# A new order of work for the first stage of an attention and mixture-of-experts layer

## The reference, cut to what matters

```python
h = tok(x)                                  # 128 batches of (375, 512): q, k, v are 125 rows each
#   weight = softmax(q.T k / sqrt(125)) over 512 positions; h = v weight.T       -> (128, 125, 512)
h = h + attn(layernorm(h), Wq, Wk, Wv, Wo)  # 8 heads of 64, 2 key/value heads, rope, softcap 50
y = layernorm(h)
h = h + (silu(y @ sw1) * (y @ sw3)) @ sw2   # shared expert, inner width 448
scores = softmax(y @ gate_w); sel = top_2(scores + expert_bias)   # 8 experts, 16000 tokens
h = h + sum over the two experts e in sel of
        (silu((y*s_e) @ w1[e]) * ((y*s_e) @ w3[e])) @ w2[e]
```

## Time and profile before

| | |
|---|---|
| median of 3 runs | 5918.14 us (5916.59 to 5921.06) |
| the profiled execution | 5922.86 us, its span 5921.1 us |
| busy of the span | PE 98%, PEld 85%, DVE 75%, ACT 52%, POOL 35% |
| first stage | about the first 62% of the span |
| second stage | about the last 37% |

### The profile page before, as it was taken

How to read it: one execution, slowest core, us unless ns; L and a number is a source line. 1 busy time by engine, 2 the same in 40 slices (tenths; PEclk the granted TensorE clock), 3 DMA queues, 4 the chain that set the end, 5 groups by cost and what they waited for, 6 DMA issues and landing times. The chain is left out here.

```text
span 5921.1 us, 109291 instructions
## 1 busy us (share of the span) xinstructions
PE 5784.0 (98%) x32259; PEld 5009.4 (85%) x32259; DVE 4450.0 (75%) x10104; ACT 3084.8 (52%) x5748; POOL 2101.8 (35%) x1711
## 2 busy tenths in 40 slices
PE   5999999999999999999999997899999999999999
PEld 4888888888888888888888886899999999999998
DVE  4888888888888888888888886666666766666665
ACT  3555555555555555555555553555555555555554
POOL 1333333333333333333333332333434444444343
PEclk8999999999999999999999999999999999999999
DMA  2111111111111111111111111777777777777762
GB/s 73 47 50 44 44 49 46 43 47 49 43 45 50 44 44 49 46 43 47 49 43 45 50 44 25 190 188 187 184 189 182 182 187 188 183 189 182 184 167 79
DMA packets 363663, 565.45 MB, mean 95 GB/s; under 512 B 92898, under 2 KB 187106, under 8 KB 363492
## 3 DMA queue, kind: packets, MB, share of 16 engines
q1 hardware_dynamic: 294276, 433.22, 24.2%
q0 software_dynamic: 69344, 131.70, 11.3%
HBM read 438.14 MB, written 138.42 MB: 97 GB/s over the span
## 5 line engine op out<-in xcount | busy, mean ns | idle before, releaser
L1438 POOL DMA_INDIRECT out_dram<-res,goal x273 | 560.8, 2054 | 1070.4 <-DMA entries<-routed_entries 480.8
L930 POOL TENSOR_SCALAR ve<-ag 125x1 f32<-125x1 f32 x256 | 56.1, 219 | 1618.3 <-DVE ag L755 942.2
L639 ACT ACTIVATE e<-ps,negmax 128x512 f32<-128x512 f32 x512 | 348.6, 685 | 513.5 <-PE ps L449 409.8
L1188 PE MATMUL ps<-rT_hi,up_hi 128*128 128x384 f32 x2548 | 552.3, 338 | 1.6 <-DVE rT_lo L1348 1.6
L1188 PE MATMUL ps<-rT_lo,up_hi 128*128 128x384 f32 x2548 | 552.1, 338 | 0.0
L1188 PE MATMUL ps<-rT_hi,up_lo 128*128 128x384 f32 x2548 | 552.0, 338 | 0.0
L1278 ACT ACTIVATE uT_hi<-egb 128x384 fp32r<-128x384 f32 x364 | 191.4, 526 | 572.3 <-DVE egb L1367 561.5
L1188 PEld LDWEIGHTS ps<-rT_hi,up_hi 128*128 128x128 f32 x2548 | 457.8, 188 | 9.8 <-issue 2.0
L1188 PEld LDWEIGHTS ps<-rT_lo,up_hi 128*128 128x128 f32 x2548 | 456.3, 188 | 0.0
L1188 PEld LDWEIGHTS ps<-rT_hi,up_lo 128*128 128x128 f32 x2548 | 456.2, 188 | 0.0
L942 POOL TENSOR_TENSOR qk_low<-X,qk_high 125x1024 fp32r<-125x1024 f32 x128 | 306.3, 2393 | 345.7 <-ACT qk_high L626 345.7
(11 more groups left out here) (220 smaller groups left out, 15549.2 us busy)
## 6 DMA issues: line engine op xcount, KB each, us to landing
raw<-in_L_ffn_w SPq DMA_DIRECT2D x182, 768.0 KB, 5.1
X<-in_x SPq DMA_DIRECT2D x128, 750.0 KB
raw<-in_L_ffn_w SPq DMA_DIRECT2D x91, 896.0 KB
raw<-in_L_ffn_w SPq DMA_DIRECT2D x273, 128.0 KB, 5.0
normed_rows<-y SPq DMA_DIRECT2D x128, 250.0 KB
out_dram<-h SPq DMA_DIRECT2D x128, 250.0 KB
rows<-normed_rows,entries POOLq DMA_INDIRECT x273
out_dram<-res,goal POOLq DMA_INDIRECT x273
```

Source lines behind the costliest of these rows:

```text
L639: nc.scalar.activation(e[:, i, :], ps[:, (i + 1) % 2, :], ACT.Exp, bias=negmax[:, i:i + 1], accum_out=total[:, i:i + 1]).then_inc(e_sb.sem, 1)
L1188: ins = nc.tensor.matmul(ps[:, bank, 0:GROUP], w[a][:, k, col:col + P], rT[b][:, k, :], start=(k == 0 and i == 0), stop=(k == KC - 1 and i ...
L1438: nc.gpsimd.indirect_dma_start(out, bass.IndirectOffsetOnAxis(ap=goal[group[1] % 2][:, i:i + 1], axis=0), res[i][:], None, bounds_check=la ...
```

## The change

It writes the streams of all five engines in the first stage in a new order. The same sums are computed.

- **PE:** the upper product, `attend(0)`, `attend(1)`, the inner turns, the whole down product and the ranks of a batch are issued one step later than before. The new order is: scores 0 and 1; upper product of `g`; scores 2 and 3; turns of v and `xn`; `attend(0)`, `attend(1)` of `f`; query product; inner turns of `g`; turn of `attn`; weights turns 0 and 1; key/value product; output product; weights turns 2 and 3; down product of `g` (11 matmuls); ranks; rope turns; high blend; turn of `y`; attention scores; low blend; gate product of `f`.
- **ACT:** the gate's tanh and the router's exp come first in the next step; the four scalings of `e`, so far on DVE, are now ACT's, after `vT_full`; the rounding of the next batch stands ahead of `e_cut_hi` 2 and 3; tanh of the attention is taken in place.
- **DVE:** gate and routing chain move to the start of the next step, between the maxima and `xT_lo`; the normalisation of `attn` follows; the second norm comes after rope; entries and places stand at the end of the step.
- **POOL:** the order is now `rstd(a)`, `vT_low`, rope sum, `rstd(f)`, `cut_scores`, scatters.
- **SP:** `y` is stored ahead of `h3`.
- The second buffer of `vaug` and the tiles `qkr` and `capped` go; some banks change.

The diff, cut to its core (PE, ACT, DVE, POOL in this order):

```diff
+                    if has(3):
+
                         pe.wait_ge(tanh_sb.sem, tanh_sb.at(f))
-                        turn(5, P, attn[:, :, :].rearrange("p a b -> p (a b)")).then_inc(aT_ps.sem, 1)
-                    if has(3):
-                        down_part(0, 1)
-                        down_part(1, 1)
+                        product(pe, ps[0:C, 7, 0:HID], yT, w3s, P, 0, HID, yT_lo.sem, yT_lo.at(g)).then_inc(up_ps.sem, 1)
+                    if has(0):
+                        scores(2)
+                        scores(3)
...
+                    if has(1):
+
+                        pe.wait_ge(xn_sb.sem, xn_sb.at(a))
+                        pe.wait_ge(place.sem, place.at(back(g, 1)))
+                        turn(3, xn).then_inc(xT_ps.sem, 1)
+                    if has(2):
+
+                        pe.wait_ge(v_sb.sem, v_sb.at(f))
+                        pe.wait_ge(gb_sb.sem, gb_sb.at(g))
+                        attend(0)
+                        pe.wait_ge(ga_sb.sem, ga_sb.at(g))
+                        attend(1)
+                    if has(1):
+
+                        pe.wait_ge(yT_lo.sem, yT_lo.at(g))
+                        pe.wait_ge(xT_hi.sem, xT_hi.at(a))
+                        product(pe, ps[0:C, 4, :], xT, wqkv, P, 0, D, xT_lo.sem, xT_lo.at(a)).then_inc(q_ps.sem, 1)
...
+                        pe.wait_ge(gb_sb.sem, gb_sb.at(g))
+                        pe.wait_ge(vT_sb.sem, vT_sb.at(t))
+                        for k in range(3):
+                            nc.tensor.transpose(ps[:, 2, k * C:(k + 1) * C], gb[0:C, k * P:(k + 1) * P],
+                                                ident[0:C, 0:C])
+                        nc.tensor.transpose(ps[0:TAIL, 2, 3 * C:4 * C], gb[0:C, 3 * P:HID],
+                                            ident[0:C, 0:C]).then_inc(hT_ps.sem, 1)
+                    if has(2):
+
+                        pe.wait_ge(attn_sb.sem, attn_sb.at(f))
+                        pe.wait_ge(xT_lo.sem, xT_lo.at(a))
+                        turn(3, attn[:, :, :].rearrange("p a b -> p (a b)")).then_inc(aT_ps.sem, 1)
+                    if has(0):
+                        turn_weights(0)
+                        turn_weights(1)
+                    if has(1):
+
+                        pe.wait_ge(tanh_sb.sem, tanh_sb.at(f))
+                        product(pe, ps[0:C, 5, 0:QKV - D], xT, wqkv, P, D, QKV, xT_lo.sem, xT_lo.at(a)).then_inc(kv_ps.sem, 1)
                     if has(2):
 
                         pe.wait_ge(aT_hi.sem, aT_hi.at(f))
                         product(pe, ps[0:C, 7, :], aT, woT, P, 0, D, aT_lo.sem, aT_lo.at(f)).then_inc(wo_ps.sem, 1)
-                    if has(1):
-
...
-                        product(pe, ps[0:C, 7, 0:HID], yT, w3s, P, 0, HID, yT_lo.sem, yT_lo.at(f)).then_inc(up_ps.sem, 1)
+                    if has(3):
+
+                        pe.wait_ge(attn_sb.sem, attn_sb.at(f))
+                        pe.wait_ge(hT_hi.sem, hT_hi.at(g))
+                        for part in range(2):
+                            for k in range(3):
+                                down_part(k, part)
+                        pe.wait_ge(hT_lo.sem, hT_lo.at(g))
+                        for part in range(2):
+                            down_part(3, part)
+                        for k in range(3):
...
                         last.then_inc(rT_ps.sem, 1)
                     if has(0):
 
@@ -567,19 +567,19 @@
                                 blend(j, 0, b)
                     if has(2):
...
+                    def soften(kv):
+
+                        act.wait_ge(s_ps.sem, s_ps.at(a, kv + 1))
+                        act.wait_ge(pv_ps.sem, pv_ps.at(f))
+                        nc.scalar.activation(prob[0:C, kv, :], ps[0:C, 5 + 2 * kv, 0:G * C], ACT.Tanh,
+                                             scale=TANH).then_inc(tanh_sb.sem, 1)
+                        act.wait_ge(tanh_sb.sem, tanh_sb.at(a, kv + 1))
+                        nc.scalar.activation(prob[0:C, kv, :], prob[0:C, kv, :], ACT.Exp,
+                                             scale=CAPF).then_inc(p_sb.sem, 1)
...
+                        act.wait_ge(rz_sb.sem, rz_sb.at(t))
+                        for i in range(KC):
+                            nc.scalar.activation(e[:, i, :], e[:, i, :], ACT.Copy,
+                                                 scale=rz[:, i:i + 1]).then_inc(e_norm.sem, 1)
...
+                    if has(-1):
+                        round_scores(back(t, -1))
                     if has(0):
                         weights_hi(2)
                         weights_hi(3)
-
-                    if has(-1):
-                        round_scores(back(t, -1))
...
+                        act.wait_ge(yT_ps.sem, yT_ps.at(f))
+                        act.wait_ge(up_ps.sem, up_ps.at(g))
+                        hi_part(yT, 4).then_inc(yT_hi.sem, 1)
+                    if has(1):
+                        soften(0)
                     if has(0):
                         act.wait_ge(o_ps.sem, o_ps.at(t))
                         act.wait_ge(h2_sb.sem, h2_sb.at(f))
                         nc.scalar.activation(h[p][0:C, :], ps[0:C, 0, :], ACT.Copy).then_inc(h_sb.sem, 1)
+                    if has(1):
+                        soften(1)
                 each_step(act, step)
...
+                    if has(3):
+                        dve.wait_ge(th_sb.sem, th_sb.at(g))
+                        dve.wait_ge(pick.sem, pick.at(back(g, 1)))
+                        nc.vector.tensor_reduce(nl[0:C, :], ps[0:C, 6, HID:HG], AX.X, ALU.max,
+                                                negate=True).then_inc(nl_sb.sem, 1)
+                    if has(0):
+                        maxima(0)
...
+
+                        dve.wait_ge(ex_sb.sem, ex_sb.at(g))
+                        nc.vector.scalar_tensor_tensor(ga[0:C, :], th[0:C, :], 1.0, ps[0:C, 6, 0:HID],
+                                                       ALU.add, ALU.mult).then_inc(ga_sb.sem, 1)
+                        dve.wait_ge(ga_sb.sem, ga_sb.at(g))
+                        dve.wait_ge(up_ps.sem, up_ps.at(g))
+                        dve.wait_ge(hT_ps.sem, hT_ps.at(back(g, 1)))
+                        nc.vector.scalar_tensor_tensor(gb[0:C, :], ga[0:C, :], 0.5, ps[0:C, 7, 0:HID],
+                                                       ALU.mult, ALU.mult).then_inc(gb_sb.sem, 1)
                     if has(0):
...
+                        chosen(nc.vector.reciprocal(rse[0:C, :], se[0:C, :]))
+                        chosen(nc.vector.tensor_scalar(sc[0:C, :], ex[0:C, :], rse[0:C, :], None, ALU.mult))
+                        chosen(nc.vector.tensor_tensor(met[0:C, :], sc[0:C, :], bias_t[0:C, :], ALU.add))
...
+                        dve.wait_ge(rank_ps.sem, rank_ps.at(back(g, 1)))
+                        nc.vector.tensor_tensor(m16[0:C, :], oh[0:C, 0, :], oh[0:C, 1, :],
+                                                ALU.add).then_inc(m16_sb.sem, 1)
+                    if has(1):
+                        dve.wait_ge(xT_hi.sem, xT_hi.at(a))
+                        lo_part(xT, 3).then_inc(xT_lo.sem, 1)
+                    if has(0):
+
+                        dve.wait_ge(e_sb.sem, e_sb.at(t))
+                        dve.wait_ge(e_norm.sem, e_norm.at(a))
+                        nc.vector.reciprocal(rz[:, :], total[:, :]).then_inc(rz_sb.sem, 1)
                     if has(2):
-
...
+                        dve.wait_ge(wo_ps.sem, wo_ps.at(f))
+                        nc.vector.tensor_tensor(h2[pf][0:C, :], ps[0:C, 7, :], h[pf][0:C, :],
+                                                ALU.add).then_inc(h2_sb.sem, 1)
...
                     if has(0):
                         weights_lo(2)
                         weights_lo(3)
                     if has(2):
-                        dve.wait_ge(ga_sb.sem, ga_sb.at(f))
-                        dve.wait_ge(up_ps.sem, up_ps.at(f))
-                        dve.wait_ge(hT_ps.sem, hT_ps.at(back(f, 1)))
-                        nc.vector.scalar_tensor_tensor(gb[0:C, :], ga[0:C, :], 0.5, ps[0:C, 7, 0:HID],
-                                                       ALU.mult, ALU.mult).then_inc(gb_sb.sem, 1)
+
+                        dve.wait_ge(rs2_sb.sem, rs2_sb.at(f))
+                        dve.wait_ge(y_out.of(back(f, 2)), y_out.at(back(f, 2)))
+                        nc.vector.tensor_scalar(y[pf][0:C, :], h2[pf][0:C, :], ag2[0:C, 0:1], rs2[0:C, :],
+                                                ALU.subtract, ALU.mult).then_inc(y_sb.sem, 1)
+                    if has(3):
+
+                        dve.wait_ge(dn_ps.sem, dn_ps.at(g))
+                        dve.wait_ge(h3_out.of(back(g, 2)), h3_out.at(back(g, 2)))
+                        nc.vector.tensor_tensor(h3[pg][0:C, :], ps[0:C, 6, :], h2[pg][0:C, :],
+                                                ALU.add).then_inc(h3_sb.sem, 1)
                     if has(1):
...
+                    if has(3):
+
```

(79 more changed lines are left out.)

358 lines of the change are left out of this document (118 added, 240 removed).

## The result

The changed kernel takes **6107.97 us** (median of 4 runs, 6103.52 to 6114.07) against 5917.88 us for the kernel before (4 runs): a ratio of 1.0321, with a 95% interval of 1.0303 to 1.0339. The forecast was 6112 us in a range of 5975 to 6205.

What follows compares the result with a forecast made beforehand. The prediction took PE's instruction stream to bound the first stage. A step of 27.5 + 0.25 + 1.75 = 29.5 us, against 27.93, times 125 gave +194 us: 6117 us profiled, 6112 us median, range 5975 to 6205.

Steps and rivals of the forecast that it cites:

- PE's stream without new waits: First stage, PE: same work, but 0.19 us routing wait and about 0.25 us smaller delays go; 27.93 becomes 27.5 us a step.
- the wait for the routing chain: PE, last piece of the down product before the rank matmul: 0.19 us of waiting for DVE goes each step.
- The scaling of e on ACT: Before PE's first weights turn: scaling moved from DVE to ACT adds a 0.25 us wait per step, between 0 and 0.6.
- The hold-up of y: End of step: POOL's cut_scores delays y on DVE; PE idles 1.75 us more before y's turn and attention scores, bounds 0 to 2.6.
- The sum: First stage: 27.5 + 0.25 + 1.75 = 29.5 us a step, 1.55 more, times 125: +194 us, median 6112 us.
- rival C: DVE: L872 stays at 1.03 us, routing chain 0.8 us longer ahead of scaling e; +100 us, 6210 us; chance 0.08.
- A: DVE: y is not held up, step 27.5 to 27.75 us, kernel faster at about 5880 us; chance 0.16.
- D: PE: the long stretch of 16 turns lowers the clock, some 4 us more per step, above 6500 us; chance 0.02.

Runs made afterwards that it cites:

- e2: Changed kernel, POOL order untouched, with y written by the same instruction plus an unread row sum (accumulator) as second output: 5893.43 us, 0.995 of the kernel before.
- e5: Kernel of e1 with the routing entries moved on DVE from behind qkT_lo to right behind hT_lo: 5881.9 us, 0.993 of the kernel before.
- e6: Kernel of e5 with POOL's two scatters moved into the next step, behind its first 1/sqrt: 5880.48 us, 0.9929 of the kernel before.
- e7: Kernel of e6 with the scaling of e back on DVE, ahead of the normalisation of attn: 5955.93 us, 1.0056 of the kernel before.
- e1: Changed kernel with one more wait: POOL's cut_scores waits until DVE has written y of the same step: 5951.94 us, 1.0049 of the kernel before.
- e4: Kernel before the change with POOL's vT_low moved directly behind the second 1/sqrt, ahead of the scatters: 6004.04 us, 1.0137 of the kernel before.
- e3: Changed kernel with the sum h3 moved behind qkT_lo on DVE: 6051.47 us, 1.0218 of the kernel before.

## Why the prediction was right, point by point

- **PE's stream without new waits, 27.5 us.** e2, e5 and e6 take 27.58, 27.57 and 27.57 a step, with the 0.14 us that PE waits for `e` in them: 27.43 without. The gain of 0.35 us on 27.93 is real. That the wait for the routing chain is part of it can be read: the down product with its ranks takes 2.69 us from start to start (1007.65 to 1010.34), and the rank matmul follows at once. How the rest divides was not tried, nor what standing together does for the turns by itself.
- **The scaling of e on ACT, 0.25 us.** 0.14 us in the changed kernel. The four took 2.56 us, as forecast from the earlier trace rows (2.55). e7 shows the move to be worth 75 us in the order of e6, which the prediction missed: it called the time taken off DVE worthless, but in the new order the normalisation is queued behind it.
- **The hold-up of y, 1.75 us.** 1.79 us in the step shown, in the two places named and by the chain named: `qk_low` starts before the 1/sqrt has ended, `y` ends 0.28 us after `qk_low`, then come h3 and qkT_lo. The stations fit as well. With K at 1004.06, where the key/value product ends and the output product starts, h2 starts at K + 3.82 (forecast 3.82), the 1/sqrt ends at K + 6.84 (6.79), `y` at K + 9.48 (9.43), and the attention scores start at K + 10.91 (10.9). Against e2, whose order is the same, the steps at full clock are 29.22 - 27.58 = 1.64 us longer. e1 takes the hold-up away in one way and e2 in another; e4 brings it into the other kernel; e3 takes away the part that stood behind `y`.
- **The sum.** 29.5 us a step was forecast; the steps at full clock take 29.22 (they alternate between 29.05 and 29.40). Of the 0.28, 0.17 are in the stream with its wait for `e` (27.75 against 27.58) and 0.11 in the hold-up. These steps give 1.29 x 125 = 161 us, 33 less than the 194 forecast. Costs that the sum had not filled more than half of it: the half clock, 13 us, and 13 us at the start of the stage, where the first `y` comes 6 us later than before and one step is 7 us longer; the end of the stage is 6 us shorter. Together that is the 181 us measured, so the profiled execution, forecast at 6117 us, took 13 us less, 6103.52. The medians lie only 4 us apart by luck: omitted costs stood against terms too high, and the profiled execution lay 4.7 us above its median before the change and 4.5 below it after. The dearer rival C, at 6210 us, lay just outside the range that was meant to reach it. DVE's last places and POOL in the long step:

```profile
154.97 2.40 POOL L929 TENSOR_TENSOR qk_low<-X,qk_high 125x1024 fp32r<-125x1024 f32 x1
161.20 0.17 DVE L905 CAST slot<-slotf 125x2 int32<-125x2 f32 x1
167.93 1.47 POOL L962 DMA_INDIRECT routed_entries<-entry,slot  x1 [10.56 <-issue]
169.71 1.21 POOL L962 DMA_INDIRECT routed_entries<-entry,slot  x1 [0.30 <-issue]
170.95 0.24 POOL L917 TENSOR_SCALAR ve<-ag 125x1 f32<-125x1 f32 x1
```

  The first scatter starts 10.6 us after `qk_low`. For 4.0 us of that the places (second row) are not yet written, as in every step; for the other 6.6 us nothing that the profile shows holds it, where later scatters start 0.95 us behind their places. The next 1/sqrt now stands behind it, `xn` comes 6 us late, PE waits and falls to half clock; that step takes 36.06 us instead of 29.2. The same stall is in e2 (7.1 us behind the places, a step of 36.24 us) and e3 (7.4 and 36.98), but not in e1 and e5 (1.1 us behind the places), where `qk_low` waits for `y`. So it does not come from `y` being held up, which it is not in e2, and it makes up most of the 12 us by which e2 is slower than e5; its cause is open.
- **The rivals.** A, a `y` that is not held up, did not happen. Its price of about 5880 us was right for one of its two forms: where the two instructions did not exclude each other, e2 took 5893 us. Where POOL's next instruction came after `y` had begun, e1 took 5952 us, since the entries then met `qk_low`; only with the entries moved as well did e5 reach 5882. C did not happen: `sc` fell to 0.23 us. D in the form given did not: across the long group of turns (1000.73 to 1002.58) the matmuls behind it keep their full-clock pitch. The rule of the Trainium skill, page "TensorE: Matmul & The Clock Gate", Part 4 (PE-mode transpose), that transposes do not count as PE activity in the same way thus brought no loss of clock behind a group of 1.8 us. Half clock came instead in some steps behind the two waits with a turn between them. The prediction had no such term.

## What to carry to other kernels

Before an order is changed on POOL, look at what it puts beside each DVE instruction that works from SBUF to SBUF. Where the DVE instruction waited for a POOL result and the next POOL instruction had its input ready, POOL's started first (1010.87 against 1011.03), and the DVE instruction ended only after it: 2.56 us instead of 0.55. A wait of POOL on that DVE result took two lines here and gave back 156 of 190 us, but the hold-up then has to be followed to the next DVE instruction of that kind. DVE instructions with an input in PSUM were not held up: `qkT_lo` took 0.68 us beside `qk_low` in e1 and 0.66 behind it in the changed kernel.

## What was not expected

- An instruction on 8 columns paid 1.25 us (e1), more than `y` costs on 512 columns when nothing holds it (0.55).
- The accumulating form of `y` takes 0.81 us against 0.55 and writes other numbers.
- POOL's first scatter started 6.6 us behind its places in the changed kernel, and 1.1 us behind them in e1, which differs by one wait.
- Two waits of 0.9 us, parted by four turns, were followed by 3.4 us at half clock in 8 of 125 steps, and one such wait alone (e3) in none; what picks the 8 steps was not found.
